# Layer-2 experts in two groups: selection of the second group between the first group's rows, sorted merges of quarters, b2 by a 16-bit product

## The chip, the cores and the metric

The kernel is one program for one core of a Trainium2 chip. The time is that of one execution on the device, in microseconds; the profile adds one execution in which the hardware recorded every instruction. Five engines run side by side and meet only through semaphores: TensorE (PE in the profile; its weight loads are listed apart as PEld), VectorE (DVE), ScalarE (ACT), GpSimd (POOL) and SyncE (SP), which here only issues DMAs.

## What is computed

The whole model is twelve residual blocks over 4096 tokens of 128 numbers. The change touches only the feed-forward block of layer 2, `l2_ffn`, which runs twice. Each of its 48 experts picks its own 128 best tokens out of all 4096:

```python
logits = xf @ Wr.T                                  # 4096 tokens x 48 experts
vals, idx = jax.lax.top_k(logits.T, cap)            # cap = 128, per expert
w = jax.nn.softmax(vals, axis=-1)
xg = xf[idx]
h = jax.nn.gelu(jnp.einsum('ecd,esdm->ecsm', xg, W1) + b1[:, None], approximate=False)
y = jnp.einsum('ecsm,esmk->ecsk', h, W2) + b2[:, None]      # s = 4 parts, k = 32 columns each
y = y.reshape(E, cap, D) * w[..., None]
out = jnp.zeros_like(xf).at[idx.reshape(-1)].add(y.reshape(-1, D))
```

`xf` is the layer norm of `x`, and the block adds half of `out` to `x`.

## The kernel before

`l2_ffn` has four stretches.

**Routing.** The layer norm of 8 chunks of 512 tokens is made on VectorE (`ln_dve`, L180), turned on TensorE (L190), kept by ScalarE (L196), and multiplied with the router's weights (L2105). ScalarE keeps the logits in `lt` (L2053): the experts lie on the partitions, tokens 0 to 2047 on partitions 0 to 47 and tokens 2048 to 4095 on partitions 64 to 111, so `lt` is 128 x 2048. The unused partitions are filled with a low number (L1961, L1962).

**Selection.** Sixteen rounds on VectorE, each of three passes over `lt`: the 8 largest (MAX8, L1969), their places (FIND_INDEX8, L1971), and their removal (MATCH_REPLACE8, L1973; not in the last round). The two halves of an expert are then merged: two small DMAs by SP bring the upper half beside the lower, one comparison picks 128 out of 256 (L1982 to L1990; this keeps the right set, in no order), ScalarE makes the exponentials (L2062), TensorE turns the lists (L2112, L2113), and VectorE writes the token numbers `from_i` and `to_i` (L1996 to L1998).

**Experts.** A pipeline over 48 experts. GpSimd gathers an expert's 128 rows (`gather`, L1935) four experts ahead and scatters the results with addition (L1947). TensorE's order in a step is `up(n + 1)`, `turn(n + 2)`, `down(n)`:

```python
pe.transpose(s.tp[:, 0, 0:P], xg[:, q, :], core.ident[:, :])                                  # turn, L2118
pe.matmul(hu[:, u, j * P:(j + 1) * P], w1[:, q, :, :].rearrange("p s m -> p (s m)")[:, j::S],  # up, L2126
          xgt[:, u, :], start=True, stop=True)
pe.matmul(yp[:, u, 0:D], h[:, u, j, :], w2b[:, q, j, :], start=j == 0, stop=j == S - 1)       # down, L2136
```

In `up` the weights of `w1` are read with a step of 4 elements (`j::S`). In `down` the activations `h` are the weights that are loaded, and 128 columns of `w2b` are moved through; `w2b` is W2 spread out with zeros by VectorE (`spread`, L2006), so that one product serves all four parts. ScalarE copies the turned rows (L2066) and applies GELU (L2073). VectorE adds b2 (L2013) and multiplies with the softmax weight (L2018); `keep` is these two. SP reloads the ring of four experts' weights (L1876, L1878) after each `down`.

**End.** SP reads both sums back in four pieces (L1904), VectorE adds them (L2035) and makes the statistics for the next block (L203).

Every wait is written by hand: `x.wait_ge(sig.sem, sig.past(n))` waits until the n-th event of that signal has happened.

## Time and profile before

| what | value |
|---|---|
| time, median of 3 runs | 3180.63 us (3173.9 to 3186.78) |
| the profiled execution's own time | 3173.69 us |
| its span | 3171.9 us |
| PE busy | 2425.3 us (76%) |
| DVE busy | 1559.8 us (49%) |
| ACT busy | 1072.4 us (34%) |
| POOL busy | 860.3 us (27%) |

Busy time is the union of an engine's instructions; the rest of the span the engine waits. These shares are means over blocks with different limits, so they say nothing of `l2_ffn` alone. The span is 1.8 us shorter than that execution's time: this much lies around it.

### The profile page before, as it was taken

To read this page: it belongs to the slowest core of one execution; us is meant where nothing else is said; L and a number is where in the kernel's file an instruction comes from. 1 tells how busy PE (TensorE), PEld (TensorE's weight loads), DVE (VectorE), ACT (ScalarE), POOL (GpSimd) and SP (SyncE) were. 2 spreads that over 40 slices of the span, in tenths; PEclk is the share of its full clock that TensorE was granted. 3 is DMA by queue.
4 is the path that set the end of the run, shared out by engine and by line. 5 is a ranking of instruction groups with operands and counts; after the bars stand their busy time and mean duration, and the time that the engine had idled before them with its cause. 6 is when DMAs were issued, how large, how long until landed. Compare 5 with 4: busy or idle time off the path is not lost. (4 is left out here: it accounts for less than half of the span.)

```text
span 3171.9 us, 45200 instructions
## 1 busy us (share of the span) xinstructions
PE 2425.3 (76%) x13236; PEld 1610.9 (51%) x13237; DVE 1559.8 (49%) x3705; ACT 1072.4 (34%) x2452; POOL 860.3 (27%) x784
## 2 busy tenths in 40 slices
PE   5979879665667313969999822968999688979998
PEld 3645556454546302955666612964444245544444
DVE  5749867544773597342334487342111577751110
ACT  1433234410341011634444311633222155662221
POOL 2535435365136402850000011851000122210000
PEclk9989879665875556989999855988999688989999
DMA  5110011457045631660000041661000333310000
GB/s 196 41 51 1 1 51 40 165 122 183 14 167 118 178 119 33 145 149 18 1 2 1 10 128 23 147 145 37 0 0 0 85 81 72 88 42 1 0 0 27
DMA packets 265331, 212.61 MB, mean 67 GB/s; under 512 B 56448, under 2 KB 245069, under 8 KB 262125
## 3 DMA queue, kind: packets, MB, share of 16 engines
q1 hardware_dynamic: 231021, 176.82, 18.8%
q0 software_dynamic: 34176, 34.09, 6.5%
q8 instruction: 73, 1.20, 0.2%
q14 instruction: 61, 0.50, 0.1%
HBM read 145.33 MB, written 64.91 MB: 66 GB/s over the span
## 5 line engine op out<-in xcount | busy, mean ns | idle before, releaser
L161 POOL TENSOR_TENSOR fields<-ln_t,power 128x4 f32<-128x4 f32 (+1 forms) x96 | 96.7, 1027 | 651.7 <-DVE ln_t L154 651.4
L2515 DVE TENSOR_TENSOR fields<-fields,s_y 128x512 f32 (+1 forms) x16 | 11.0, 687 | 496.8 <-PE s_y L2594 496.8
L2579 PE MATMUL s_z<-s_ha,s_wt_h 128*128 128x512 f32 x512 | 222.4, 592 | 0.0
L2586 PE MATMUL s_z<-s_hb,s_wt_h 128*128 128x512 f32 x512 | 222.3, 592 | 0.0
L2805 DVE TENSOR_REDUCE s_mx<-s_sa 128x2 f32<-128x512 f32 x256 | 167.1, 685 | 65.2 <-PE s_sa L2958 63.6
L2126 PE MATMUL s_hu<-s_xgt,s_w 128*128 128x128 f32 x768 | 195.4, 400 | 1.7 <-issue 1.7
L2886 ACT ACTIVATE s_e<-s_sc 128x512 f32<-128x512 f32 x256 | 149.9, 599 | 127.1 <-PE s_sc L2974 125.4
L2126 PEld LDWEIGHTS s_hu<-s_xgt,s_w 128*128 128x128 f32 x768 | 186.7, 327 | 3.0 <-issue 3.0
L2112 PE MATMUL s_lp<-ident,s_posf 48*128 48x48 f32 x2 | 0.6, 312 | 233.3 <-DVE s_prob L1994 233.3
L190 PE MATMUL s_tp<-ident,xn 128*128 128x128 f32 x288 | 60.6, 348 | 143.5 <-DVE xn L180 140.5
L1935 POOL DMA_INDIRECT s_xg<-rows_dram,s_from_i x96 | 95.5, 995 | 268.6 <-DVE s_to_i L1998 240.0
L1947 POOL DMA_INDIRECT acc_dram<-s_yo,s_to_i x96 | 153.3, 1597 | 41.6 <-issue 29.0
L2586 PEld LDWEIGHTS s_z<-s_hb,s_wt_h 128*128 128x128 f32 x512 | 97.4, 190 | 122.4 <-issue 122.4
L2579 PEld LDWEIGHTS s_z<-s_ha,s_wt_h 128*128 128x128 f32 x512 | 96.3, 190 | 115.7 <-issue 115.7
L2958 PE MATMUL s_sa<-s_kx,s_qx 72*128 72x256 bf16 x512 | 113.1, 308 | 39.1 <-DVE s_mx L2805 21.3
L190 PEld LDWEIGHTS s_tp<-ident,xn 128*128 128x128 f32 x288 | 44.1, 184 | 170.0 <-DVE xn L180 140.2
L2112 PEld LDWEIGHTS s_lp<-ident,s_posf 48*128 48x128 f32 x2 | 0.4, 180 | 234.9 <-issue 234.9
L2570 PE MATMUL s_z<-xnt,s_wt_w 128*128 128x512 f32 x256 | 112.7, 593 | 4.6 <-ACT s_wt_w L2529 4.6
L2013 DVE TENSOR_TENSOR s_yb<-s_yp,s_b 128x128 f32<-128x128 f32 x96 | 28.0, 291 | 175.5 <-issue 110.0
L2236 DVE TENSOR_SCALAR s_den<-s_kn 128x8 f32<-128x8 f32 x64 | 10.3, 160 | 210.9 <-PE s_kn L2397 210.9
L2226 POOL TENSOR_TENSOR s_rd<-s_rv,s_power 128x2 f32<-128x2 f32 x16 | 11.1, 697 | 371.6 <-DVE s_rv L2260 371.6
L196 ACT ACTIVATE xnt<-s_tp 128x512 f32<-128x512 f32 x72 | 43.0, 597 | 201.5 <-PE s_tp L190 193.6
(458 smaller groups left out, 6039.0 us busy)
## 6 DMA issues: line engine op xcount, KB each, us to landing
s_w<-in_L_ffn_W_dram SPq DMA_DIRECT2D x96, 256.0 KB
acc_dram<-s_zero SPq DMA_DIRECT2D x32, 512.0 KB, 5.9
s_kx<-k_dram SPq DMA_DIRECT2D x16, 576.0 KB
s_qx<-q_dram SPq DMA_DIRECT2D x48, 192.0 KB
fields<-acc_dram SPq DMA_DIRECT2D x16, 512.0 KB, 7.2
table_dram<-s_table_rows SPq DMA_DIRECT2D x2, 3136.0 KB, 9.2
s_wg<-in_L_ffn_w_gate_dram SPq DMA_DIRECT2D x64, 96.0 KB
s_wu<-in_L_ffn_w_up_dram SPq DMA_DIRECT2D x64, 96.0 KB
```

The costliest lines, as they stand in the source:

```text
L161: pool.tensor_tensor(core.rstd[:, tiles], core.ln_t[:, 2, tiles], core.power[:, 0:CT], ALU.pow).then_inc(s.scale_ready.sem, 1)
L190: last = pe.transpose(s.tp[:, u % s.tp_banks, j * P:(j + 1) * P], core.xn[:, u, j, :], core.ident[:, :])
L196: act.activation(core.xnt[:, u, :], s.tp[:, u % s.tp_banks, :], ACT.Copy).then_inc(s.xnt_ready.sem, 1)
L1935: pool.indirect_dma_start(xg[:, n % RING, :], None, table, bass.IndirectOffsetOnAxis(ap=from_i[:, n:n + 1], axis=0)).then_inc(xg_loaded[n ...
L1947: pool.indirect_dma_start(sums, bass.IndirectOffsetOnAxis(ap=to_i[:, n:n + 1], axis=0), yo[:, n % RING, :], None, compute_op=ALU.add).then ...
L2126: last = pe.matmul(hu[:, u, j * P:(j + 1) * P], w1[:, q, :, :].rearrange("p s m -> p (s m)")[:, j::S], xgt[:, u, :], start=True, stop=True)
L2570: pe.matmul(z[:, (2 * f + half) % 4, :], wt[m][:, 0, f * P:(f + 1) * P], core.xnt[:, u, :], start=True, stop=True).then_inc(group_done.sem, 1)
L2579: last = pe.matmul(z[:, o, :], wt["h1"][:, f, o * P:(o + 1) * P], ha[:, f, :], start=f == 0, stop=f == HB - 1)
L2586: last = pe.matmul(z[:, o, :], wt["h2"][:, f, o * P:(o + 1) * P], hb[:, f, :], start=f == 0, stop=f == HB - 1)
L2805: dve.tensor_reduce(mx[:, i, t, 2 * pairs:2 * pairs + 2], sa[:, n % 2, :, :], AX.X, ALU.max).then_inc(max_done.sem, 1)
L2886: act.activation(e[:, n % RING, :, :], sc[:, n % 2, :, :], ACT.Exp).then_inc(exp_done.sem, 1)
L2958: last = pe.matmul(sa[:, n % 2, a, :], qx[0:ROWS, slot, h, t * P:(t + 1) * P], kx[0:ROWS, slot, h, :], start=True, stop=True)
```

## The change

The router's logits are laid out anew: four quarters of 1024 tokens on partitions 0 to 31, 32 to 63, 64 to 95 and 96 to 127, for 32 experts at a time. So there are two groups, of 32 and of 16 experts (the second is padded with repeated experts up to 32), and two products a chunk in the routing. VectorE selects for group 0 in sixteen rounds over 128 x 1024, merges quarters pairwise by DMA, sorts the merged lists with a bitonic network of seven steps (`sort_step`; equal values go by token number), and merges once more. Then the experts start; the 47 passes and the merges of group 1 stand between the `keep`s of experts 0 to 29 in VectorE's order. GpSimd gathers the first four experts of group 1 at steps 30 and 31.

Besides this: W1 is loaded so that `up` reads its weights densely; W2 of all 48 experts is loaded once, in packets of 128 bytes, and `down` moves 32 columns a part with no spreading; b2 is split into three 16-bit parts and enters by one bf16 product of 3 rows; the normalized rows go straight to `all_xn` (GpSimd's copies L1923 go); loops are written out; and the rows of x, the table and the sums lie in DRAM partition by partition, so that their packets are 4 KB and more in place of 512 bytes.

```diff
+    LANES = 32
+    PARTS = P // LANES
+    PART = TOKENS // PARTS
+    GROUPS = ((0, LANES), (LANES, EXPERTS - LANES))
+    ROUNDS = CAP // TOP
+    STEPS = 7
     LOW = -3.0e38
...
+            def load(n):
+                sp.dma_start(w1[:, n % RING, :, :], w["L2_ffn_W1"][n].rearrange("s d m -> d s m")).then_inc(ring_loaded[n % RING].sem, 16)
...
+            with nc.allow_non_contiguous_dma("the second weights of a part of a row"):
+                for e in range(0, EXPERTS, 8):
+                    sp.dma_start(w2[:, e:e + 8, :, :].rearrange("p e s k -> p (e s) k"),
+                                 w["L2_ffn_W2"][e:e + 8].rearrange("e s m k -> m (e s) k")).then_inc(w2_loaded.sem, 16)
...
+                if n in (0, LANES):
+                    pool.wait_ge(index_ready.sem, index_ready.past(n // LANES))
...
-                if n + RING < EXPERTS:
+                if n + RING < LANES or LANES <= n < EXPERTS - RING:
                     gather(n + RING)
+                if n == LANES - 2:
+                    gather(LANES)
+                    gather(LANES + 1)
+                if n == LANES - 1:
+                    gather(LANES + 2)
+                    gather(LANES + 3)
...
+            def round_part(g, k):
+                r = k // 3
+                got = lists[:, 0, r * TOP:(r + 1) * TOP]
+                data = lt[:, g, :, :].rearrange("p i w -> p (i w)")
+                if k % 3 == 0:
+                    dve.max(got, data)
+                    dve.drain()
+                if k % 3 == 1:
+                    dve.max_index(pos[:, r * TOP:(r + 1) * TOP], got, data)
+                if k % 3 == 2 and r < ROUNDS - 1:
+                    dve.match_replace(data, got, data, LOW)
+                    dve.drain()
...
+            def sort_step(j):
+                n = 3 * LANES
+                far = CAP // 2 >> j
+
+                def half(buf, field, side):
+                    return merge[0:n, buf, field, :].rearrange("p (b two w) -> p b two w", two=2, w=far)[:, :, side, :]
+
+                def wide(t, which=0):
+                    return t[0:n, which * (CAP // 2):(which + 1) * (CAP // 2)].rearrange("p (b w) -> p b w", w=far)
+
+                a, b = j % 2, 1 - j % 2
+                va, vb, pa, pb = half(a, 0, 0), half(a, 0, 1), half(a, 1, 0), half(a, 1, 1)
+                dve.tensor_tensor(wide(level), va, vb, ALU.is_equal)
+                dve.tensor_tensor(wide(before), pa, pb, ALU.is_lt)
+                dve.tensor_tensor(wide(above), va, vb, ALU.is_gt)
+                dve.tensor_tensor(wide(step), pa, pb, ALU.subtract)
+                dve.drain()
+                dve.tensor_tensor(wide(level), wide(level), wide(before), ALU.mult)
+                dve.tensor_tensor(half(b, 0, 0), va, vb, ALU.max)
+                dve.tensor_tensor(half(b, 0, 1), va, vb, ALU.min)
+                dve.drain()
+                dve.tensor_tensor(wide(above), wide(above), wide(level), ALU.add)
+                dve.drain()
+                dve.tensor_tensor(wide(step), wide(step), wide(above), ALU.mult)
+                dve.drain()
+                dve.tensor_tensor(half(b, 1, 0), pb, wide(step), ALU.add)
+                last = dve.tensor_tensor(half(b, 1, 1), pa, wide(step), ALU.subtract)
+                if j == STEPS - 1:
+                    last.then_inc(sorted_ready.sem, 1)
+                dve.drain()
...
+            def keep(n):
+                u = n % 2
+                dve.wait_ge(y_done.sem, y_done.past(n))
+                if n >= RING:
+                    dve.wait_ge(added[u].sem, 16 * ((n - RING) // 2 + 1))
+                dve.tensor_scalar(yo[:, n % RING, :], lp[:, u, 0:D], prob_s[:, n:n + 1], None, ALU.mult).then_inc(y_kept.sem, 1)
...
+            dve.wait_ge(logits_kept.sem, logits_kept.past(1))
+            for k in range(3 * ROUNDS):
+                round_part(0, k)
+            put_lists()
+            merge_pairs(0)
+            for j in range(STEPS):
+                sort_step(j)
+            merge_last(0)
+            weigh(0)
+            place(0)
+            dve.drain()
+            dve.wait_ge(logits_kept.sem, logits_kept.past(3))
+            for n in range(EXPERTS):
+                keep(n)
+                for k in range(min(9 * n // 4, 3 * ROUNDS), min(9 * (n + 1) // 4, 3 * ROUNDS)):
+                    round_part(1, k)
+                if n == 21:
+                    put_lists()
+                if n == 22:
+                    merge_pairs(1)
+                    sort_step(0)
+                if n == 23:
+                    sort_step(1)
+                    sort_step(2)
...
-            def spread(n, ring, q):
-                dve.wait_ge(ring_loaded[q].sem, ring * 32 + 32)
-                dve.wait_ge(y_done.sem, y_done.past(n - RING))
-                dve.tensor_tensor(w2b[:, q, :, :].rearrange("p j (s k) -> p j s k", s=S),
-                                  w2[:, q, :, :].unsqueeze(2).to_broadcast([P, S, S, K]),
-                                  own[:, :].unsqueeze(1).unsqueeze(3).to_broadcast([P, S, S, K]), ALU.mult).then_inc(w2_spread.sem, 1)
...
-                pe.matmul(lp[:, u, :], wr[:, :], core.xnt[:, u, :], start=True, stop=True).then_inc(routed.sem, 1)
...
+                for g in range(2):
+                    last = pe.matmul(lp[lanes, 2 * g + c % 2, :], wr[:, g * LANES:(g + 1) * LANES], core.xnt[:, c % 2, :],
+                                     start=True, stop=True)
+                last.then_inc(routed.sem, 1)
...
-                    last = pe.matmul(hu[:, u, j * P:(j + 1) * P], w1[:, q, :, :].rearrange("p s m -> p (s m)")[:, j::S],
-                                     xgt[:, u, :], start=True, stop=True)
+                    last = pe.matmul(hu[:, u, j * P:(j + 1) * P], w1[:, n % RING, j, :], xgt[:, u, :], start=True, stop=True)
...
-                pe.wait_ge(w2_spread.sem, w2_spread.past(n))
+            def down(n):
+                u = n % 2
                 pe.wait_ge(gelu_done.sem, gelu_done.past(n))
-                pe.wait_ge(y_kept.sem, y_kept.past(n - 2))
+                if n >= 2:
+                    pe.wait_ge(y_kept.sem, y_kept.past(n - 2))
+                pe.matmul(lp[:, u, 0:D], ones_b[:, :], b2[:, n, :], start=True, stop=False)
                 for j in range(S):
-                    last = pe.matmul(yp[:, u, 0:D], h[:, u, j, :], w2b[:, q, j, :], start=j == 0, stop=j == S - 1)
+                    last = pe.matmul(lp[:, u, j * K:(j + 1) * K], h[:, u, j, :], w2[:, n, j, :], start=False, stop=j == S - 1)
                 last.then_inc(y_done.sem, 1)
...
+                if n == 28:
+                    turn_slots(1)
```

TensorE's order in the middle of the expert pipeline. `s_xg` is the gathered rows, `s_hu` the output of `up`, `s_yp` (before) and `s_lp` (after) that of `down`; the shapes are those of the output. Before, a step and a bit:

```order
L2126 MATMUL s_hu<-s_xgt,s_w 128x128 x4
L2118 MATMUL s_tp<-ident,s_xg 128x128
L2136 MATMUL s_yp<-s_w2b,s_h 128x128 x4
L2123 REGISTER_ALU
L2126 MATMUL s_hu<-s_xgt,s_w 128x128 x4
```

Of the change:

```order
L2270 MATMUL s_hu<-s_xgt,s_w 128x128 x4
L2261 MATMUL s_tp<-ident,s_xg 128x128
L2278 MATMUL s_lp<-s_b,s_ones_b 128x128
L2280 MATMUL s_lp<-s_w,s_h 128x32 x4
L2270 MATMUL s_hu<-s_xgt,s_w 128x128 x4
```

The order of the step is the same; each `down` has one product more, and its four large ones write 32 columns in place of 128.

VectorE's order in the experts. Before, `keep` is two instructions and `spread` one:

```order
L2006 TENSOR_TENSOR s_w2b<-s_w,s_own 128x512
L2013 TENSOR_TENSOR s_yb<-s_yp,s_b 128x128
L2018 TENSOR_SCALAR s_yo<-s_yb,s_prob_s 128x128
L2006 TENSOR_TENSOR s_w2b<-s_w,s_own 128x512
L2013 TENSOR_TENSOR s_yb<-s_yp,s_b 128x128
```

Of the change, from the end of group 0's lists on (`s_lists` and `s_lt` are the lists and the logits of a group):

```order
L2104 TENSOR_SCALAR s_to_i<-s_lp 128x16
L2112 TENSOR_SCALAR s_yo<-s_lp,s_prob_s 128x128
L2015 MAX s_lists<-s_lt 128x8
L2018 MAX_INDEX s_pos<-s_lists,s_lt 128x8
L2112 TENSOR_SCALAR s_yo<-s_lp,s_prob_s 128x128
L2020 MATCH_REPLACE s_lt<-s_lists,s_lt 128x1024
L2015 MAX s_lists<-s_lt 128x8
L2112 TENSOR_SCALAR s_yo<-s_lp,s_prob_s 128x128
L2018 MAX_INDEX s_pos<-s_lists,s_lt 128x8
L2020 MATCH_REPLACE s_lt<-s_lists,s_lt 128x1024
```

`keep` is one instruction now, and two or three passes over group 1's logits stand behind each of them, up to expert 21; the merges follow at experts 21 to 29.

TensorE's order in the routing, the end of a chunk; before and then of the change:

```order
L190 MATMUL s_tp<-ident,xn 128x128 x4
L2105 MATMUL s_lp<-xnt,s_wr 128x512
```

```order
L2231 MATMUL s_tp<-ident,all_xn 128x128 x4
L2242 MATMUL s_lp<-xnt,s_wr 32x512 x2
```

A chunk has two products of 512 moving columns where it had one.

## Rows read from the trace of the kernel before

**Rows 1.** Stretches (from:to, length): routing, selection, lists, experts, end; the second execution whole

```profile
core 0: us, PE busy (x) PEld busy (x) DVE busy (x) ACT busy (x) POOL busy (x), PEclk, DMA share, GB/s
1101.60:1124.40 22.80, 16.10 (x55) 8.47 (x55) 15.03 (x41) 9.70 (x19) 14.09 (x20) 0.68 0.87 279
1124.40:1235.10 110.70, 0.00 (x0) 0.00 (x0) 108.31 (x79) 1.30 (x2) 0.00 (x0) 0.51 0.14 41
1235.10:1241.60 6.50, 0.42 (x2) 0.29 (x2) 2.75 (x15) 0.50 (x2) 0.02 (x1) 0.50 0.04 10
1241.60:1402.70 161.10, 146.54 (x816) 141.07 (x816) 57.66 (x144) 92.61 (x262) 124.29 (x96) 0.96 0.61 129
1402.70:1422.30 19.60, 0.00 (x0) 0.00 (x0) 11.48 (x36) 0.00 (x0) 0.00 (x0) 0.50 0.85 214
1819.20:2141.30 322.10, 163.55 (x873) 149.39 (x873) 196.12 (x314) 104.24 (x284) 138.68 (x116) 0.74 0.47 111
```

**Rows 2.** Timeline, POOL in the experts: start us, us, engine, line, op, count, [idle before <-releaser]

```profile
1306.92 0.98 POOL L1935 DMA_INDIRECT s_xg<-rows_dram,s_from_i  x1 [0.30 <-PE s_tp L2118]
1308.21 1.59 POOL L1947 DMA_INDIRECT acc_dram<-s_yo,s_to_i  x1 [0.30 <-issue]
```

**Rows 3.** Timeline, weight loads of one step of the experts at the full clock

```profile
1254.95 1.95 PEld L2126 LDWEIGHTS s_hu<-s_xgt,s_w 128*128 128x128 f32 x8
1256.69 0.27 PEld L2118 LDWEIGHTS s_tp<-ident,s_xg 128*128 128x128 f32 x1
1256.92 0.97 PEld L2136 LDWEIGHTS s_yp<-s_w2b,s_h 128*128 128x128 f32 x8
1257.82 0.31 PEld L2126 LDWEIGHTS s_hu<-s_xgt,s_w 128*128 128x128 f32 x1
```

**Rows 4.** Timeline, the end: a sum over 1024 columns on VectorE

```profile
1408.66 1.22 DVE L2035 TENSOR_TENSOR fields<-fields,s_acc_b 128x1024 f32<-128x1024 f32 x1 [9.86 <-DMA s_acc_b<-acc_dram]
```

**Rows 5.** Timeline, from the lists to the first gather and the first turn

```profile
1238.04 0.28 DVE L1982 TENSOR_TENSOR s_first<-s_vals 48x128 f32<-48x128 f32 x1 [2.50 <-DMA s_posf<-s_posf]
...
1238.52 0.28 DVE L1985 TENSOR_TENSOR s_posf<-s_posf 48x128 f32<-48x128 f32 x1
1238.87 0.28 DVE L1987 TENSOR_TENSOR s_posf<-s_posf,s_first 48x128 f32<-48x128 f32 x1
...
1241.58 1.09 POOL L1935 DMA_INDIRECT s_xg<-rows_dram,s_from_i  x1 [119.85 <-DVE s_to_i L1998]
...
1244.25 0.18 PEld L2118 LDWEIGHTS s_tp<-ident,s_xg 128*128 128x128 f32 x1 [3.55 <-DMA s_xg<-rows_dram,s_from_i]
```

**Rows 6.** Timeline, layer 1: an element by element operation on 64 columns

```profile
724.96 0.22 DVE L1375 TENSOR_TENSOR s_hp<-s_gs,s_gu 96x64 f32<-96x64 f32 x1 [1.77 <-issue]
```

**Rows 7.** Timeline, the router's product at the full clock: two records, one product

```profile
1117.52 1.02 PE L2105 MATMUL s_lp<-xnt,s_wr 128*128 128x512 f32 x2
```

**Rows 8.** Timeline, weight loads at the low clock: expert 0's `down`, and layer 0's router

```profile
1250.40 1.78 PEld L2136 LDWEIGHTS s_yp<-s_w2b,s_h 128*128 128x128 f32 x8 [0.34 <-issue]
...
390.74 1.83 PEld L664 LDWEIGHTS s_yp<-s_wr,xnt 128*128 128x128 f32 x8
392.31 0.90 PEld L190 LDWEIGHTS s_tp<-ident,xn 128*128 128x128 f32 x4
393.19 1.83 PEld L664 LDWEIGHTS s_yp<-s_wr,xnt 128*128 128x128 f32 x8
```

**Rows 9.** The same view as rows 1: layer 0's router, layer 1's experts, layer 2's experts

```profile
389.00:406.00 17.00, 16.22 (x81) 15.96 (x79) 7.67 (x32) 4.26 (x8) 4.99 (x6) 0.50 0.32 132
700.00:760.00 60.00, 48.08 (x246) 44.53 (x246) 21.87 (x74) 8.27 (x38) 48.43 (x39) 0.50 0.67 140
1252.60:1314.00 61.40, 58.83 (x336) 57.07 (x336) 23.96 (x60) 38.61 (x107) 49.28 (x38) 1.00 0.67 146
```

**Rows 10.** Page, the DMA queue of SP: packets, MB, share of 16 engines

```profile
q1 hardware_dynamic: 231021, 176.82, 18.8%
```

**Rows 11.** Timeline, ScalarE at the start of the experts

```profile
1245.06 1.28 ACT L2066 ACT_TABLE_LOAD   x1
```

More of the change, by code:

```diff
@@ L1892, in _ @@
[L1892 to L1899 removed]
+                tiles = slice(n * 8, (n + 1) * 8)
+                sp.dma_start(region_rows(1)[:, tiles, :], zero[:, :, :]).then_inc(zeroed.sem, 16)
@@ new lines, in move, with move2 @@
+            def move(g):
+                sp.wait_ge(best_found.sem, best_found.past(g))
+                sp.dma_start(other[0:LANES, :, :], lists[LANES:2 * LANES, :, :]).then_inc(moved.sem, 16)
+                sp.dma_start(other[2 * LANES:3 * LANES, :, :], lists[3 * LANES:P, :, :]).then_inc(moved.sem, 16)
+            def move2(g):
+                sp.wait_ge(sorted_ready.sem, sorted_ready.past(g))
+                sp.dma_start(other2[:, :, :], merge[2 * LANES:3 * LANES, 1, :, :]).then_inc(moved2.sem, 16)
@@ L1900, in _ @@
+            move(0)
+            move2(0)
+            for n in range(EXPERTS - RING):
+                sp.wait_ge(y_done.sem, y_done.past(n))
+                load(n + RING)
+                if n == 20:
+                    move(1)
+                if n == 26:
+                    move2(1)
             for q in range(2):
@@ L2026, in _, with normal @@
-            dve.wait_ge(b2_loaded.sem, 16)
-            spread(0, 0, 0)
-            ring_body(0, False)
-            with dve.Fori(1, EXPERTS // RING - 1) as ring:
-                ring_body(ring)
-            ring_body(EXPERTS // RING - 1, last=True)
+            def normal(c):
+                dve.wait_ge(s.scale_ready.sem, s.scale_ready.past(c))
+                for t in range(c * CT, (c + 1) * CT):
+                    last = dve.tensor_scalar(core.all_xn[:, t, :], core.x[:, t, :], core.mean[:, t:t + 1], core.rstd[:, t:t + 1],
+                                             ALU.subtract, ALU.mult)
+                last.then_inc(xn_ready.sem, 1)
@@ new lines, in _ @@
+            dve.drain()
+            dve.tensor_copy(offset[:, :], offset_i[:, :])
+            for c in range(2, CHUNKS):
+                normal(c)
+            cut_b2()
+            dve.wait_ge(logits_kept.sem, logits_kept.past(1))
[8 more added lines that the diff above has]
+            place(0)
@@ L2072, in gelu @@
                 for j in range(S):
-                    last = act.activation(h[:, u, j, :], hu[:, u, j * P:(j + 1) * P], ACT.Gelu, bias=b1[:, j, bass.ds(n, 1)])
+                    last = act.activation(h[:, u, j, :], hu[:, u, j * P:(j + 1) * P], ACT.Gelu, bias=b1[:, j, n:n + 1])
                 last.then_inc(gelu_done.sem, 1)
-            turn(0, 0)
-            def ring_body(n0, last=False):
-                for q in range(RING):
-                    if not (last and q == RING - 1):
-                        turn(n0 + q + 1, q + 1)
-                    gelu(n0 + q, q)
@@ L2084, in _ @@
-            with act.Fori(0, EXPERTS // RING - 1) as ring:
-                ring_body(ring * RING)
-            ring_body(EXPERTS - RING, True)
+            exp(0)
+            turn(0)
+            for n in range(EXPERTS):
+                if n + 1 < EXPERTS:
+                    turn(n + 1)
+                gelu(n)
+                if n == 28:
+                    exp(1)
         @block.tensor
@@ new lines, in turn_slots, with turn @@
+            def turn_slots(g):
+                pe.wait_ge(listed.sem, listed.past(g))
+                for a in range(2):
+                    last = pe.transpose(slots(g)[:, a, :], final[:, a, :], core.ident[0:LANES, 0:LANES])
+                last.then_inc(slots_turned.sem, 1)
+            pe.wait_ge(logits_kept.sem, logits_kept.past(3))
+            turn_slots(0)
+            pe.wait_ge(b2_placed.sem, 48)
+            pe.wait_ge(w2_loaded.sem, 16 * (EXPERTS // 8))
+            def turn(n):
+                pe.wait_ge(xg_loaded[n % RING].sem, 16 * (n // RING + 1))
+                if n >= 1:
+                    pe.wait_ge(xt_kept.sem, xt_kept.past(n - 1))
+                pe.transpose(tp[:, 0, 0:P], xg[:, n % RING, :], core.ident[:, :]).then_inc(xt_done.sem, 1)
@@ L2151, in _ @@
-            with pe.Fori(0, EXPERTS // RING - 1) as ring:
-                ring_body(ring * RING, ring)
-            ring_body(EXPERTS - RING, EXPERTS // RING - 1, True)
+            turn(0)
+            up(0)
+            turn(1)
+            for n in range(EXPERTS):
+                if n + 1 < EXPERTS:
+                    up(n + 1)
+                if n + 2 < EXPERTS:
+                    turn(n + 2)
+                down(n)
+                if n == 28:
+                    turn_slots(1)
 def l2_attn(core):
```

356 lines of the change are left out of this document (179 added, 177 removed).

## The prediction

> **What bounds the kernel now.** I read the stretches first, since the page's shares mix blocks with different limits. An execution of `l2_ffn` takes 320.7 us of the span (1101.6 to 1422.3) and the second 322.1 [rows 1]: 643 of 3171.9 us. Each stretch has one limit. In the selection VectorE works 108.3 of 110.7 us, alone. The lists are a chain of 6.5 us between engines. In the experts (161.1 us) both TensorE and GpSimd are nearly full, 146.5 and 124.3 us. The timeline then shows the two loops: GpSimd needs 0.30 + 0.98 for a gather and 0.30 + 1.59 for a scatter, 3.17 us an expert [rows 2]; TensorE at its full clock needs 2.87 us, from 1254.95 to 1257.82, of which `up` takes 1.74, `turn` 0.23 and `down` 0.90 [rows 3]. So GpSimd sets the pace, with TensorE close behind, as long as the clock is at its upper level: the stretch has a granted share of 0.96 [rows 1].
>
> **Selection.** The 108.3 us are 47 passes of 2.30 us over 2048 columns [rows 1]. The trace has no pass over 1024 columns. Another VectorE operation takes 1.22 us for 1024 [rows 4], as a column per cycle with a small fixed part would, so I take 1.24 for a pass. Group 0 costs 47 x 1.24 plus the gaps that stay (2.4 us), 60.7 us: **-50 us** an execution. The bounds are 1.15 (half of 2.30) and 1.35.
>
> **Lists of group 0.** 6.5 us now. New are seven sort steps, one merge and one more move by DMA. A step has eleven operations on 96 x 64, 0.22 us each [rows 6], with five drains; a dependent operation starts its own length + 0.07 after the last one's start (1238.52 to 1238.87) [rows 5], and independent ones overlap a little. That is 2.3 us, 16.2 for seven. A second move costs about what the first does, 2.50 us of waiting [rows 5]; the second merge with its index arithmetic about twelve operations of 0.2, 2.5. Together **+21 us**, between 16 and 26. Nothing hides it.
>
> **Routing.** VectorE loses the low fills, GpSimd its copies, but TensorE has two products of 512 columns a chunk in place of one. A product is two records in 1.02 us, a little less in a row since the last one's tail overlaps [rows 7]; eight more are some 7 us at the upper clock, and TensorE was busy 16.1 of 22.8 us [rows 1]. I take **+5 us**, from +2 to +9 by how early the clock rises.
>
> So the first gather comes 24 us earlier. Up to here the change gains.
>
> **Experts, GpSimd and VectorE.** GpSimd's 3.17 us stay. VectorE gets, for 22 experts, 2.25 passes x 1.24 + 0.3 for `keep` = 3.1, with drains 3.2 us; `spread` goes. The passes are queued ahead of the next `keep`, three of them at worst 3.8 us, and `down(n + 2)` and the scatter wait for a `keep`, but with two experts of slack. Neither gives a pace above 3.3 us.
>
> **Experts, TensorE, the term that decides.** At the upper clock dense weights bring `up` from 1.74 to 0.90 as `down` has [rows 3]; `down` keeps its 0.90, since its eight weight loads stay although it moves a quarter of the columns, and gets one bf16 product (0.1). That is 2.1 us, no longer a limit. But this stretch starts after VectorE's long stretch alone, at the low level. There `down` needs 1.78 us for its eight loads [rows 8], 0.21 to 0.22 each. That a load with few columns behind it costs the same at this level, layer 0's router shows: eight loads with 8 moving columns and four with 128 take 2.45 us, 0.204 each (390.74 to 393.19) [rows 8]. So at 1.2 GHz: 8 x 0.213 for `up`, 8 x 0.213 for `down`, 0.23 for `turn`, 0.12 for the bias: **3.76 us an expert**, above the 3.17 of GpSimd. The new loop is slower than the old one unless the clock rises.
>
> Does it? Before, it does: from 1252.6 on the share is 1.00, with TensorE busy 58.8 of 61.4 us and 128 columns moved per 128-column load [rows 9]. In layer 0's router TensorE is as full, 16.2 of 17.0 us, but eight of twelve loads have 8 columns behind them, and the share stays 0.50 through the stretch; in layer 1's experts it stays 0.50 for 60 us, TensorE busy 48.1, with 64 columns in half its products [rows 9]. The new loop is of that kind: half of its loads have 32 columns behind them. I take it that the clock stays at 1.2 GHz.
>
> The Trainium skill (TensorE: Matmul & The Clock Gate, Why this matters for your kernels) says that keeping TensorE continuously busy brings the full clock. Here the trace differs: 16.2 of 17.0 us busy went with 0.50 [rows 9]. By the page the pace would be GpSimd's, and the sum that of the first rival below.
>
> **Sum of the experts at the low clock.** First gather to first turn 2.7 us (1241.58 to 1244.25) [rows 5], 0.9 more to `up(0)`, 48 x 3.76 = 180.5, about 1.5 for the first experts' dependences, and 4.6 from the last `down` to the stretch's end, both as now. The change of groups costs a hole: `turn_slots(1)` waits for `weigh(1)`, which waits for an exponential behind `gelu(28)` with its table load of 1.28 us and another back to GELU [rows 11], then `place(1)`, the gather (2.7 us) and `turn(32)`: some 4.5 us of idle TensorE at expert 29 and 3.5 at 30, together 8, where nothing covers it. Total 198 against 161.1: **+37 us**.
>
> **End.** Packets of 4 KB in place of 512 bytes; VectorE works only 11.5 of 19.6 us there [rows 1]. **-2 us**, between 0 and -5.
>
> **Sum.** -50 + 21 + 5 + 37 - 2 = +11 us an execution, +21 us for two: 3173.7 + 21 = 3195 on the profiled execution's own time. That one lies 7 us under the median of 3180.6, which gives 3202; I say **3200 us**.
>
> **Rivals.**
> *The clock rises in the new loop* (0.14). For it: the loop before it did so, and TensorE would be full at the low level. Against it: [rows 9]. Then GpSimd and VectorE set 3.2 us, and with the hole the experts are some 9 us longer than now: -50 + 21 + 5 + 9 - 2 = -17 an execution, 3145 us. This is the case on the other side. The sign turns at 3.76 - 11/48 = 3.53 us an expert.
> *VectorE or the 128-byte packets of W2 bind* (0.08). A pass over 1024 that took 1.6 us would make 22 experts 0.3 us slower than the 3.76 and add 17 us to the selection: some 22 an execution, 3244 us. W2 has 24,576 packets, 1536 for each of 16 engines; the queue's mean is 41 ns a packet (0.188 x 16 x 3171.9 us / 231021) [rows 10], which gives 63 us from the routing's end on, some 1126, as group 0's lists are done at 1124.4 + 5 + 60.7 = 1190. It binds from 42 ns for the first move in the same queue, and from 58 ns for the first turn; at 80 ns it would cost some 33 us an execution, 3266. Smaller packets should take less than the mean.
> *It gains nothing and loses nothing* is the lower half of the likeliest case: a pace of 3.6 us and short lists.
>
> **Numbers.** Low clock 0.78, of it range 3175 to 3228 (pace 3.7 to 3.95, lists and routing +-5 each). A measurement of this kernel can tell about 0.5%, 16 us. Low clock: slower 0.48, same 0.28, faster 0.02. High clock: faster 0.14. The binding rival: slower 0.06, same 0.02. Together slower 0.54, same 0.30, faster 0.16. The range 3148 to 3230 holds most of the low case and the upper half of the fast one.
>
> **What would show it.** In the profile after: PEclk 0.5 through the experts; `up` and `down` weight loads of 0.21 us spacing; steps of 3.8 us with GpSimd waiting for VectorE's `yo`, VectorE for TensorE; the first gather 24 us earlier; passes of 1.24 us; a hole of 8 us near expert 30. It is wrong if the share is 1.0 there: then steps of 3.2 us and a time near 3145.

## The result, and the profile after

The changed kernel takes **3215.7 us** (median of 4 runs, 3209.5 to 3216.6), the kernel before, run beside it, 3182.0 us (3173.9 to 3186.8): a ratio of 1.0112, 95% interval 1.0093 to 1.0130. It is 34 us, about 1.1%, slower, which is more than the 0.5% a measurement can tell. The forecast was 3200 us, slower, with a range of 3148 to 3230. The profiled executions stand further apart, 3213.7 against 3171.9 us of span, since that of before, 3173.7 us, was faster than all four runs.

The stretches of the first execution of `l2_ffn` after, which begins 2.7 us later in the span than before: routing, group 0's selection, its lists, experts, end; the last row is the second execution whole. They answer to [rows 1].

```profile
core 0: us, PE busy (x) PEld busy (x) DVE busy (x) ACT busy (x) POOL busy (x), PEclk, DMA share, GB/s
1104.30:1131.10 26.80, 22.25 (x69) 7.67 (x69) 11.26 (x46) 6.52 (x14) 9.64 (x12) 0.82 0.85 285
1131.10:1191.60 60.50, 0.00 (x0) 0.00 (x0) 58.17 (x78) 2.22 (x3) 0.00 (x0) 0.53 0.55 51
1191.60:1219.40 27.80, 0.39 (x2) 0.28 (x2) 18.33 (x101) 0.49 (x2) 0.00 (x0) 0.50 0.02 4
1219.40:1431.50 212.10, 200.20 (x866) 177.89 (x866) 91.18 (x227) 67.49 (x245) 123.45 (x96) 0.50 0.42 85
1431.50:1448.90 17.40, 0.00 (x0) 0.00 (x0) 11.48 (x36) 0.00 (x0) 0.00 (x0) 0.50 0.75 242
1842.00:2186.40 344.40, 222.65 (x937) 185.84 (x937) 190.47 (x487) 76.73 (x263) 132.99 (x108) 0.53 0.46 96
```

| us, one execution | before | after | difference | forecast |
|---|---|---|---|---|
| routing | 22.8 | 26.8 | +4.0 | +5 |
| selection (group 0) | 110.7 | 60.5 | -50.2 | -50 |
| lists (group 0) | 6.5 | 27.8 | +21.3 | +21 |
| experts | 161.1 | 212.1 | +51.0 | +37 |
| end | 19.6 | 17.4 | -2.2 | -2 |
| sum | 320.7 | 344.6 | +23.9 | +11 |

The second execution went from 322.1 to 344.4, +22.3. The two give 46 us; the spans differ by 42, so the other blocks of this one execution were 4 us shorter, which I leave as what single executions differ by.

The experts' granted share fell from 0.96 [rows 1] to 0.50. A step of their loop after, weight loads alone (each row: start, length, engine, line, tile, shape, count, idle time before):

```profile
1263.17 1.83 PEld L2270 LDWEIGHTS s_hu<-s_xgt,s_w 128*128 128x128 f32 x8
1264.88 0.23 PEld L2261 LDWEIGHTS s_tp<-ident,s_xg 128*128 128x128 f32 x1
1265.44 0.10 PEld L2278 LDWEIGHTS s_lp<-s_b,s_ones_b 3*128 3x128 bf16 x1 [0.33 <-issue]
1265.65 1.78 PEld L2280 LDWEIGHTS s_lp<-s_w,s_h 128*128 128x128 f32 x8
1267.31 1.83 PEld L2270 LDWEIGHTS s_hu<-s_xgt,s_w 128*128 128x128 f32 x8
```

A step is 1267.31 - 1263.17 = **4.14 us**, where the forecast had 3.76: `up` 1.71, from `turn` to the bias 0.56, from the bias to `down` 0.21, `down` 1.66. The engines behind TensorE wait in each step. GpSimd waits for `s_yo`:

```profile
1264.15 1.59 POOL L1983 DMA_INDIRECT acc_dram<-s_yo,s_to_i  x1 [1.31 <-DVE s_yo L2112]
...
1267.61 0.35 DVE L2112 TENSOR_SCALAR s_yo<-s_lp,s_prob_s 128x128 f32<-128x128 f32 x1 [1.24 <-PE s_lp L2280]
```

and VectorE, even with passes queued, waits for `down` (the second row is a `keep`). The waits run back to TensorE, which is busy without a gap. Here are fifty us out of the loop:

```profile
1240.00:1290.00 50.00, 50.00 (x220) 44.58 (x218) 37.10 (x60) 15.74 (x60) 31.19 (x25) 0.50 0.46 97
```

TensorE's row is 50.00 of 50.00 us and the granted share still 0.50.

The selection and the lists went as worked out. A pass over 1024 columns takes 1.21 to 1.23 us, a round of three passes 3.85 (1131.10 to 1134.95), and a sort step 2.46 (1196.22 to 1198.68) in place of 2.3, which is 1 us more for seven that the rest of the lists gave back. The wait for the first move, 2.52 us, is the 2.50 of [rows 5], so W2's packets did not hold it up:

```profile
1131.10 1.23 DVE L2015 MAX8 s_lists<-s_lt 128x8 f32<-128x1024 f32 x1 [12.89 <-ACT s_lt L2179]
...
1134.95 1.23 DVE L2015 MAX8 s_lists<-s_lt 128x8 f32<-128x1024 f32 x1
...
1194.73 0.29 DVE L2031 TENSOR_TENSOR s_above<-s_lists,s_other 96x128 f32<-96x128 f32 x1 [2.52 <-DMA s_other<-s_lists]
...
1196.22 0.22 DVE L2057 TENSOR_TENSOR s_level<-s_merge 96x64 f32<-96x64 f32 x1
...
1198.68 0.22 DVE L2057 TENSOR_TENSOR s_level<-s_merge 96x64 f32<-96x64 f32 x1
```

The group change, by TensorE's weight loads from the `up` of expert 29 on:

```profile
1341.83 1.83 PEld L2270 LDWEIGHTS s_hu<-s_xgt,s_w 128*128 128x128 f32 x8
...
1347.08 0.29 PEld L2249 LDWEIGHTS s_tp<-ident,s_final 32*128 32x128 f32 x2 [0.99 <-DVE s_final L2095]
1347.43 1.78 PEld L2270 LDWEIGHTS s_hu<-s_xgt,s_w 128*128 128x128 f32 x8
...
1351.53 1.83 PEld L2270 LDWEIGHTS s_hu<-s_xgt,s_w 128*128 128x128 f32 x8
1356.92 0.18 PEld L2261 LDWEIGHTS s_tp<-ident,s_xg 128*128 128x128 f32 x1 [3.57 <-DMA s_xg<-rows_dram,s_from_i]
...
1359.20 0.97 PEld L2270 LDWEIGHTS s_hu<-s_xgt,s_w 128*128 128x128 f32 x4
```

The `up`s stand 5.60, 4.10 and 7.67 us apart (the view ends inside the last one, so that it shows only four of its eight loads). Over 4.14 that is 1.5 for the turn of the lists and 3.5 for the first gather: 5.0 us in all, not 8.

### The profile page after: what moved, and what is told of

Same layout as the page of the kernel before. It is cut to its first block and busy times, and to the rows that moved or that the text cites. A ratio compares the mean times of both kernels' runs of the same rounds, so it can differ in the third digit from the quotient of the medians.

```text
span 3213.7 us, 44096 instructions
## 1 busy us (share of the span) xinstructions
PE 2542.3 (79%) x13364; PEld 1682.2 (52%) x13365; DVE 1552.8 (48%) x4051; ACT 1017.8 (32%) x2410; POOL 848.2 (26%) x768
## 5 line engine op out<-in xcount | busy, mean ns | idle before, releaser
L161 POOL TENSOR_TENSOR fields<-ln_t,power 128x4 f32<-128x4 f32 x96 | 96.5, 1031 | 648.2 <-DVE ln_t L154 648.2
L2280 PE MATMUL s_lp<-s_w,s_h 128*128 128x32 f32 x768 | 183.9, 404 | 0.0
L2280 PEld LDWEIGHTS s_lp<-s_w,s_h 128*128 128x128 f32 x768 | 170.9, 327 | 11.2
L2270 PEld LDWEIGHTS s_hu<-s_xgt,s_w 128*128 128x128 f32 x768 | 175.1, 333 | 3.2 <-issue 3.1
L190 PE MATMUL s_tp<-ident,xn 128*128 128x128 f32 x224 | 46.4, 344 | 131.9 <-DVE xn L180 130.1
L2112 DVE TENSOR_SCALAR s_yo<-s_lp,s_prob_s 128x128 f32<-128x128 f32 x96 | 33.7, 351 | 225.7 <-PE s_lp L2280 223.6
L2197 ACT ACTIVATE s_xgt<-s_tp 128x128 f32<-128x128 f32 x96 | 26.6, 277 | 271.7 <-PE s_tp L2261 271.7
L2205 ACT ACTIVATE s_h<-s_hu,s_b 128x128 f32<-128x128 f32 x384 | 109.2, 374 | 5.3 <-PE s_hu L2270 5.2
```

The source lines that it names most:

```text
L161: pool.tensor_tensor(core.rstd[:, tiles], core.ln_t[:, 2, tiles], core.power[:, 0:CT], ALU.pow).then_inc(s.scale_ready.sem, 1)
L2205: last = act.activation(h[:, u, j, :], hu[:, u, j * P:(j + 1) * P], ACT.Gelu, bias=b1[:, j, n:n + 1])
L2270: last = pe.matmul(hu[:, u, j * P:(j + 1) * P], w1[:, n % RING, j, :], xgt[:, u, :], start=True, stop=True)
L2280: last = pe.matmul(lp[:, u, j * K:(j + 1) * K], h[:, u, j, :], w2[:, n, j, :], start=False, stop=j == S - 1)
```

## The experiments

What was open: whether the clock, and the 32 columns, are the cause (theory A) or VectorE, GpSimd and the group change would hold the loop at that length anyway (B); and what makes the step 4.14 and not 3.76 us. The table puts them together. "Experts" is from the first gather to the first load of the end stage, with its granted share, in the first execution.

| kernel | median us | ratio to before (95%) | experts us | share |
|---|---|---|---|---|
| after | 3215.7 | 1.0112 (1.0093-1.0130) | 212.1 | 0.50 |
| e1_wide | 3144.9 | 0.9889 (0.9859-0.9919) | 173.8 | 0.88 |
| e2_before_narrow | 3243.5 | 1.0181 (1.0136-1.0226) | 190.0 | 0.50 |
| e4_no_bias | 3181.5 | 1.0008 (0.9991-1.0026) | 190.4 | 0.50 |
| e5_passes_ahead | 3307.8 | 1.0399 (1.0369-1.0429) | 257.8 | 0.50 |
| e6_diag | 3149.9 | 0.9887 (0.9851-0.9924) | 174.1 | 0.88 |
| e7_before_dense | 3182.3 | 0.9986 (0.9963-1.0009) | 161.6 | 0.93 |
| e8_diag_order | 3146.2 | 0.9861 (0.9823-0.9899) | 173.2 | 0.87 |
| e9_fp32_bias | 3263.4 | 1.0252 (1.0203-1.0302) | 224.1 | 0.55 |
| e10_rows128 | 3185.0 | 1.0009 (0.9991-1.0027) | 198.8 | 0.50 |
| e11_wide_start | 3201.2 | 1.0070 (1.0047-1.0093) | 203.6 | 0.55 |
| e12_earlier | 3147.8 | 0.9898 (0.9860-0.9935) | 171.8 | 0.91 |
| e13_move_later | 3141.0 | 0.9874 (0.9854-0.9894) | 170.8 | 0.88 |

### e1_wide: the same products, 128 columns wide

```diff
-                    last = pe.matmul(lp[:, u, j * K:(j + 1) * K], h[:, u, j, :], w2[:, n, j, :], start=False, stop=j == S - 1)
+                    last = pe.matmul(lp[:, u, 0:D], h[:, u, j, :], w2[:, n, :, :], start=False, stop=j == S - 1)
```

> The changed kernel, but each product of `down` moves the whole 128 columns of its expert's W2 and adds them into the whole 128 columns of `s_lp`, in place of its own part's 32 into its own 32. So the sum over the parts is another computation than the reference's; loads, products and waits are as many as in the changed kernel. Theory A (the 32 columns keep TensorE's clock at 1.2 GHz, and the clock sets the pace): the granted share goes to 1.00 after the first experts, a step from 4.14 to some 3.2 us (GpSimd's 3.17), the experts from 212 to about 168 us, the whole to about 3128 us. Theory B (VectorE's passes, GpSimd or the group change hold the loop anyway): the share may rise, but the stretch stays within 10 us of 212 and the time within 3195 to 3215 us. Theory C (nothing moves the clock here, and wide products only cost): no change, 3215 us.

Measured 3144.9 us, 71 less than the changed kernel for moving four times the columns in `down`. A's direction and mechanism hold, its size is 17 us too hopeful. The loads and GpSimd in the loop:

```profile
1266.91 0.14 PEld L2261 LDWEIGHTS s_tp<-ident,s_xg 128*128 128x128 f32 x1 [0.95 <-DMA s_xg<-rows_dram,s_from_i]
1267.17 0.09 PEld L2278 LDWEIGHTS s_lp<-s_b,s_ones_b 3*128 3x128 bf16 x1
1267.33 0.97 PEld L2280 LDWEIGHTS s_lp<-s_w,s_h 128*128 128x128 f32 x8
1268.21 0.97 PEld L2270 LDWEIGHTS s_hu<-s_xgt,s_w 128*128 128x128 f32 x8
```

```profile
1267.58 0.99 POOL L1965 DMA_INDIRECT s_xg<-rows_dram,s_from_i  x1 [0.30 <-PE s_tp L2261]
1268.87 1.59 POOL L1983 DMA_INDIRECT acc_dram<-s_yo,s_to_i  x1 [0.30 <-issue]
1270.77 0.99 POOL L1965 DMA_INDIRECT s_xg<-rows_dram,s_from_i  x1 [0.31 <-issue]
```

Both `up` and `down` take 0.89 us, TensorE waits for a gather, and GpSimd goes from one gather to the next in 3.19 us with no wait beyond its 0.30: the limit has changed hands. What A had left out stands in the windows of the same stretch:

```profile
1226.00:1290.00 64.00, 52.67 (x373) 45.02 (x372) 60.34 (x95) 26.49 (x102) 50.64 (x40) 0.96 0.59 126
1290.00:1325.00 35.00, 23.01 (x149) 19.56 (x149) 23.55 (x110) 14.03 (x48) 22.17 (x17) 0.88 0.50 98
1325.00:1350.00 25.00, 18.87 (x110) 16.46 (x110) 2.41 (x10) 7.99 (x32) 15.94 (x13) 0.77 0.43 94
```

In 1226 to 1290 GpSimd is busy 50.6 of 64 us, which is full at its 0.30 per instruction, and VectorE is nearly as full, 60.3; from 1290 to 1350 GpSimd is not, and the share dips. That is where VectorE merges group 1's lists between `keep`s and where the groups change.

### e2_before_narrow: the columns alone, in the old kernel

```diff
-                    last = pe.matmul(yp[:, u, 0:D], h[:, u, j, :], w2b[:, q, j, :], start=j == 0, stop=j == S - 1)
+                    last = pe.matmul(yp[:, u, j * K:(j + 1) * K], h[:, u, j, :], w2b[:, q, j, j * K:(j + 1) * K], start=True, stop=True)
```

> The kernel before, but each product of `down` moves only the 32 columns of its part's block in `s_w2b` and writes them to its part's 32 columns; `spread` and everything else stay, and the result is the same. Theory A: the granted share stays at 0.50 through the experts; a step is `up` 1.80 + `turn` 0.60 + `down` 1.66 = 4.06 us as at expert 0 of the kernel before, the stretch 161 becomes about 206 us, the time about 3180 + 90 = 3270 us. Theory B: less is moved, TensorE's weight loads stay 0.90 for `down` at the upper clock, and the time stays at 3180 us.

3243.5 us, 63 us more than before for a quarter of the columns, at a share of 0.50 throughout. The step is 3.76 us (1257.22 to 1260.98):

```profile
1257.22 0.25 PEld L2118 LDWEIGHTS s_tp<-ident,s_xg 128*128 128x128 f32 x1
1257.45 1.83 PEld L2136 LDWEIGHTS s_yp<-s_w2b,s_h 128*128 128x128 f32 x8
1259.16 1.97 PEld L2126 LDWEIGHTS s_hu<-s_xgt,s_w 128*128 128x128 f32 x8
1260.98 0.25 PEld L2118 LDWEIGHTS s_tp<-ident,s_xg 128*128 128x128 f32 x1
```

A foresaw 4.06, with 0.60 for `turn` as at expert 0 of the kernel before. In the running loop `turn` takes 0.23; the 0.34 us at expert 0 is no part of it. Theory B, by which less work can't cost, falls. With e1 this shows the cause from both sides: in the old loop and in the new one the share is 0.50 with 32 columns behind half of the loads, and 0.96 and 0.88 with 128 (e9 and e11 below have a short exception at the start of the experts).

### e5_passes_ahead: VectorE's passes out of the loop

```diff
             dve.wait_ge(logits_kept.sem, logits_kept.past(3))
+            for k in range(3 * ROUNDS):
+                round_part(1, k)
+            put_lists()
             for n in range(EXPERTS):
                 keep(n)
-                for k in range(min(9 * n // 4, 3 * ROUNDS), min(9 * (n + 1) // 4, 3 * ROUNDS)):
-                    round_part(1, k)
-                if n == 21:
-                    put_lists()
```

> The changed kernel with all 47 passes of group 1 done before the first `keep` in place of between the `keep`s of experts 0 to 20; the merges stay where they are. GpSimd and TensorE start as before and run into the buffers' limits after a few experts, so some 60 us are added ahead. Theory A (TensorE at the low clock sets the pace): the step stays 4.14 us from then on, and the time is about 3215 + 2 x 55 = 3325 us. Theory B (VectorE's passes set or share the pace of the first 21 experts): their step falls well below 4.14 once the passes are gone, by up to 0.9 us each, and the time is about 3290 us.

3307.8 us, 92 more, with the stretch 45.7 us longer. The step without passes is 4.14 us as with them (`turn` at 1292.13 and 1296.27), and TensorE is full again:

```profile
1290.00:1340.00 50.00, 50.00 (x220) 44.62 (x219) 4.21 (x12) 15.74 (x60) 31.82 (x25) 0.50 0.48 97
```

So in the changed kernel the passes cost the steps nothing, and standing between them they save 46 us an execution. The time alone would not decide: 3307.8 us lies halfway between A's 3325 and B's 3290, but the step is A's. My estimate of 55 took too little off for the three experts that TensorE does ahead.

### e4_no_bias, e9_fp32_bias, e10_rows128: the missing 0.38 us

e4 drops the product `ones_b` x `b2`. e9 makes `b2` one row of 32 bits, e10 128 rows of 16 bits:

```diff
-        b2 = s.sb("b2", [3, EXPERTS, D], BF16)
-        ones_b = s.sb("ones_b", [3, P], BF16)
+        b2 = s.sb("b2", [P, EXPERTS, D], BF16)
+        ones_b = s.sb("ones_b", [P, P], BF16)
```

> The changed kernel without the 16-bit product of the bias (b2 is left out of the result; the four parts of `down` each start their own columns). Theory D (the 0.33 us in which TensorE stands idle in each step comes with the 16-bit product): a step goes from 4.14 to 4.14 - 0.21 - 0.33 = 3.60 us, 26 us less an execution, about 3163 us. Theory E (the idle time stands behind `turn`, whatever comes next, as at expert 0 of the kernel before, where a transposition at 1.2 GHz took 0.60 us up to the next load): only the product's 0.21 go, step 3.93, about 3195 us. In both the clock stays at 0.50.

> The changed kernel, but the bias enters by one 32-bit product of one row (a row of ones and b2 as it is) in place of one 16-bit product of three rows. Without a bias product the step was 3.63 us, with the 16-bit one 4.14. Theory D (the idle 0.33 us comes with the change between 32 and 16 bits): the step is 3.63 + two weight loads of 0.21 = 4.05 us, about 3206 us. Theory H (any small extra product brings the idle time): 4.38 us, about 3238 us.

> The changed kernel, but the 16-bit product of the bias has 128 rows in place of 3 (rows 3 to 127 are zeros), so it loads and moves full height. An execution pays some us more ahead of the experts for the fill. Theory I (the idle time comes with the step from 128 rows to few and back): the step is 3.63 + 0.1 to 0.2 = 3.75 to 3.85 us. Theory D (it comes with the change to 16 bits): the step stays 4.14 us. The granted share stays 0.50 in both.

e4: the step is 3.63 us (`turn` at 1262.16 and 1265.79), the idle time is gone with the product, and the time is that of the kernel before. D was right on the step and E fell. On the time D missed: it had 3163 us, and 3181.5 lies between that and E's 3195. A part of this stands in the trace: the stretch is 21.7 us shorter and not 26, since the two steps of the group change now cost 7.5 us over the others, where they cost 5.1 in the changed kernel. The rest is the spread of this kernel's runs, 3171 to 3190 us, of which the profiled one is the fastest.

e9 refutes D's reason. Its product is of 32 bits like its neighbours, and the step is 4.65 us (1261.18 to 1265.83), longer than D's 4.05 and than H's 4.38, with idle time on both sides:

```profile
1261.18 0.23 PEld L2261 LDWEIGHTS s_tp<-ident,s_xg 128*128 128x128 f32 x1
1261.75 0.50 PEld L2278 LDWEIGHTS s_lp<-s_b,s_ones_b 1*128 1x128 f32 x2 [0.33 <-issue]
1262.47 1.78 PEld L2280 LDWEIGHTS s_lp<-s_w,s_h 128*128 128x128 f32 x8 [0.23 <-issue]
```

e10 has the 16 bits but full height, and no idle time:

```profile
1263.53 0.23 PEld L2263 LDWEIGHTS s_tp<-ident,s_xg 128*128 128x128 f32 x1
1263.74 0.15 PEld L2280 LDWEIGHTS s_lp<-s_b,s_ones_b 128*128 128x128 bf16 x1
1263.96 1.83 PEld L2282 LDWEIGHTS s_lp<-s_w,s_h 128*128 128x128 f32 x8
1265.67 1.83 PEld L2272 LDWEIGHTS s_hu<-s_xgt,s_w 128*128 128x128 f32 x8
1267.37 0.23 PEld L2263 LDWEIGHTS s_tp<-ident,s_xg 128*128 128x128 f32 x1
```

Its step is 3.84 us. Theory I holds for the three rows: with the type as it was and 128 rows, the idle time is gone and the step 0.30 us shorter. That one row of 32 bits pays for the same reason is likely, but no run fills it up, so its part isn't shown. The 125 rows of zeros save 31 us of the whole (3185.0 against 3215.7).

### e11_wide_start: does the clock stay up once it is up?

As e1_wide for `n < 6` alone, the narrow products from 6 on.

> The changed kernel with the wide products (128 columns, every part into the whole output: another computation of the same size for these experts) for the experts 0 to 5 alone, and the narrow ones from 6 on. Theory A: the clock rises during the first experts as it did with wide products throughout, and falls back to 1.2 GHz some experts after the narrow ones begin; from there the step is 4.14 us, and the whole gains 5 to 20 us on 3215. Rival (once up, the clock stays up as long as TensorE has work): about 3145 us.

3201.2 us, 15 less. Consecutive stretches:

```profile
1235.00:1245.00 10.00, 8.42 (x64) 7.10 (x62) 9.48 (x16) 4.17 (x16) 8.17 (x7) 1.00 0.62 132
1245.00:1255.00 10.00, 8.23 (x43) 7.07 (x43) 9.56 (x17) 3.73 (x15) 8.17 (x7) 0.68 0.63 118
1255.00:1265.00 10.00, 10.00 (x46) 9.10 (x45) 7.43 (x12) 2.82 (x11) 6.60 (x7) 0.50 0.47 93
1265.00:1300.00 35.00, 35.00 (x154) 30.97 (x153) 26.39 (x41) 11.06 (x43) 22.17 (x18) 0.50 0.46 99
```

The first narrow `down` begins at 1245.86, and by 1249.86 its loads are at the low level's spacing again. But the wide products did not start this rise: the share leaves 0.50 between 1228 and 1229, and the first wide `down` begins at 1229.48. e9, narrow throughout, has the same rise in its first execution:

```profile
1227.00:1247.00 20.00, 18.23 (x134) 15.72 (x132) 16.94 (x27) 9.80 (x38) 13.94 (x11) 1.00 0.52 113
1248.00:1443.00 195.00, 186.83 (x762) 164.25 (x762) 73.09 (x200) 55.26 (x203) 104.15 (x80) 0.50 0.40 79
```

e10 and e5 have one of 10 and 6 us at the start of their second executions; the changed kernel, e2 and e4 have none. Why some executions rise there and others don't stays open. What all the narrow ones share is that the share, once down, stays at 0.50 to the end of the experts, while in e6, which has wide products, it dips at the group change and is back at 1.00 from 1337 to 1343. So the rival falls: a high clock did not last with narrow products. What the six wide experts themselves were worth isn't shown.

### e7_before_dense: what dense weights bring alone

```diff
-                    last = pe.matmul(hu[:, u, j * P:(j + 1) * P], w1[:, q, :, :].rearrange("p s m -> p (s m)")[:, j::S],
+                    last = pe.matmul(hu[:, u, j * P:(j + 1) * P], w1[:, q, j, :],
```

> The kernel before, but `up` reads its weights densely, w1[:, q, j, :] in place of every fourth column (so hidden units are paired with other rows of W2: another computation of the same size). Theory F (GpSimd's 3.17 us set the step at the full clock): TensorE's step falls from 2.87 to about 2.05 us, and the time stays within 5 us of 3180. Theory G (TensorE had a share in the step): the stretch of 161 us loses some 0.2 us an expert, about 3160 us.

3182.3 us, no difference, as F said. TensorE's busy time fell from 146.5 [rows 1] to 109.8 us, GpSimd's stayed at 124.3, and the stretch at 161.6. The share was 0.93 with 128 columns behind every load, though TensorE was idle for a third of the time; in e2, with 32 behind half of them, it was 0.50 with TensorE busy 182.0 of 190.0 us. So in these runs the share does not go by how long TensorE is busy:

```profile
1242.04:1403.67 161.63, 109.76 (x816) 100.09 (x816) 58.11 (x144) 92.40 (x262) 124.27 (x96) 0.93 0.63 128
```

### e6_diag, e8_diag_order, e12_earlier, e13_move_later: a version that is faster

e6 gives the reference's result with wide products: GpSimd zeroes the slots at the start, and zeros stand beside each block of W2.

```diff
-        w2 = s.sb("w2", [P, EXPERTS, S, K])
+        w2 = s.sb("w2", [P, RING, S * (D + K)])
...
+                    sp.dma_start(w2[:, n % RING, :].rearrange("p (s d) -> p s d", s=S)[:, :, 0:K],
+                                 w["L2_ffn_W2"][n].rearrange("s m k -> m s k")).then_inc(ring_loaded[n % RING].sem, 16)
...
-                    last = pe.matmul(lp[:, u, j * K:(j + 1) * K], h[:, u, j, :], w2[:, n, j, :], start=False, stop=j == S - 1)
+                    last = pe.matmul(lp[:, u, 0:D], h[:, u, j, :], w2[:, n % RING, j * D:(j + 1) * D], start=False, stop=j == S - 1)
```

e8, in TensorE's loop (`LANES` is 32):

```diff
+                if n == LANES - 1:
+                    down(n)
                 if n + 1 < EXPERTS:
                     up(n + 1)
+                if n == LANES - 2:
+                    down(n)
                 if n + 2 < EXPERTS:
                     turn(n + 2)
-                down(n)
+                if n not in (LANES - 2, LANES - 1):
+                    down(n)
```

e12, VectorE's part, and SP's, where e13 has 19 in place of 17:

```diff
-                for k in range(min(9 * n // 4, 3 * ROUNDS), min(9 * (n + 1) // 4, 3 * ROUNDS)):
+                for k in range(min(5 * n // 2, 3 * ROUNDS), min(5 * (n + 1) // 2, 3 * ROUNDS)):
...
+                if 19 <= n < 19 + STEPS:
+                    sort_step(n - 19)
...
-                if n == 20:
+                if n == 17:
                     move(1)
```

> The changed kernel with W2 in a ring of four experts, loaded with W1 of the same expert (in packets of 128 bytes) into the diagonal blocks of zeroed slots, so that each product of `down` moves 128 columns, of which 96 are zeros, and the result is the reference's. By theory A as the kernel with wide products showed it: the clock goes to 1.00 in the experts, the stretch takes about 174 us, and the time is 3145 us. If the packets of 128 bytes of each expert don't land within a step (3.2 us), TensorE waits for the weights and the time is above 3180 us.

> The kernel of e6_diag, and in TensorE's order `down` of experts 30 and 31 stands ahead of the `turn` of experts 32 and 33, so that these two scatters don't wait for group 1's first gather. Expected: the hole at the group change gets some 4 us shorter, 8 us less than e6_diag in all, about 3137 us. If the chain from the exponential to the gather sets the hole alone, it stays as in e6_diag.

> The kernel of e6_diag with group 1's work brought forward: 2.5 passes behind each `keep` in place of 2.25, one sort step behind each of the experts 19 to 25, the last merge, the exponential, the turn and the placing one expert earlier each, and the gathers of experts 32 and 33 at step 29. The first 19 experts then go at VectorE's pace (2.5 x 1.24 + 0.35 + gaps = 3.6 us in place of 3.2, 8 us more), and the merges, which in e6_diag held the scatters up from expert 22 on, fit into GpSimd's step. Expected: the index of group 1 some 12 us earlier, the hole gone, 5 us less an execution, about 3138 us. Rival: what is gained at the group change is lost in the first 19 experts, 3148 us.

> The kernel of e12_earlier, but in SP's order the move of group 1's lists stands behind the weight load issued at step 19 in place of step 17. In e12_earlier SP's queue stood at that move from 1287.8 to 1298.1 us, with the loads of three experts behind it, and TensorE waited 6.06 us for weights at expert 22. Expected: that wait is gone, 5 us less an execution, about 3138 us. Rival: GpSimd, which had waited only 3.6 us there, catches up anyway and the time stays within 3 us of 3148.

e6 came as expected, 3149.9 us: 66 us below the changed kernel and 1.1% below the one before. e8, 3146.2, can't be told from it, and its stretch is 0.9 us shorter, not 4: the chain to group 1's gather holds. In e12 the hole at the group change shrank (8.0 us between two `turn`s in e6, 1324.96 to 1332.99; here the `up`s are at most 5.8 apart, 1320.68 to 1326.44), but the time stayed. Two losses stand against the gain. From the `turn` of expert 0 to that of expert 19, where each `keep` has 2.5 passes behind it, e12 takes 63.1 us and e6 58.3, as the rival said. And SP's queue stood at the move of group 1's lists, with the weights of three experts behind it:

```profile
1287.27 0.51 SPq L1907 DMA_DIRECT2D s_w<-in_L_ffn_W_dram  x1
1298.14 0.52 SPq L1926 DMA_DIRECT2D s_other<-s_lists  x1
```

```profile
1303.20 1.78 PEld L2258 LDWEIGHTS s_hu<-s_xgt,s_w 128*128 128x128 f32 x8 [6.06 <-DMA s_w<-in_L_ffn_W_dram]
```

e13 moves it two steps back. That wait is gone from its trace, but it was worth only about 1 us: from the `turn` of expert 0 to that of expert 32 e13 takes 112.4 us and e12 113.4, since TensorE now waits for gathers (3.1 us before the `turn` at 1304.49, 2.5 before that at 1309.74). The stretches say the same, 170.8 against 171.8. The 5 us an execution that I expected aren't shown: 3141.0 us (0.9874, 0.9854 to 0.9894) is the lowest median of the study, but its interval and e12's overlap, and the rival, by which GpSimd catches up anyway, fits the trace better. That e13 beats both kernels, by 1.3% and 2.3%, is shown.

## Why the prediction was right, and where its terms were off

**What bounds the kernel before: right.** GpSimd sets the pace there: e7 takes 37 us of work from TensorE and the time doesn't move.

**Selection -50, lists +21, routing +5, end -2: right**, with -50.2, +21.3, +4.0 and -2.2. The estimate of 1.24 us for a pass was 0.02 above the rows.

**The clock stays at 1.2 GHz: right, and shown.** It was argued from [rows 9] alone, by likeness; e1 and e2 change only the columns, and the share follows each time. In the changed kernel itself it is 0.50 through the experts of both executions. The forecast's reason does not cover the rises at the start that e9, e10 and e5 have. The Trainium skill (TensorE: Matmul & The Clock Gate, Why this matters for your kernels) has it that continuous work brings the full clock. By that rule the time would have been the first rival's 3145 us. The trace doesn't agree: 50.00 of 50.00 us busy went with 0.50. The rival's time was well priced, though: e1 and e6, which do have the clock, measured 3145 and 3150 us.

**The step of 3.76 us: the mis-sized term.** "0.12 for the bias" was the product's own length. With it comes 0.3 us of idle time because it has 3 rows. From `turn` to `down` 0.77 us passed in place of 0.35, and 48 x 0.38 = 18 us an execution. Without the bias the step was 3.63 us against the forecast's 3.64. This term alone is why the kernel is slower rather than equal: e10, with full height and the clock as low, takes 3185.0 us against 3179.3 for the kernel before, a ratio of 1.0009.

**The hole of 8 us: 5.0.** I had charged 4.5 us to the turn of the lists; it cost 1.5, since most of the exponential's chain (its table loaded at 1341.39, itself at 1345.01) ran beside `down` of expert 28. That hangs on the step: counted by the `turn`s, the same two steps cost 5.1 us over the others here, 5.9 at 3.84 us a step (e10) and 7.5 at 3.63 (e4), so for its own step of 3.76 the forecast was nearer than the 5.0 says.

**Sum.** +18 for the step, -3 for the hole and -1 for the rest make the experts +51 in place of +37, and an execution +24 in place of +11. For both executions that is 46 in place of 21 us, 25 more, and the median is 16 above the forecast: the other blocks were 4 us shorter, the 7 us between profiled execution and median, which the forecast carried over, weren't there after the change (3215.5 and 3215.7), and rounding 3202 to 3200 took 2 the other way.

**Where luck helped.** The step of 4.14 us lies outside the 3.7 to 3.95 that the forecast gave the low clock. With it and all else as forecast, the sum is 3202 + 96 x 0.38 = 3238 us, above the range; the smaller hole, the other blocks and those 7 us brought the time back inside. The sign was helped too: e10, whose step of 3.84 us is the nearest to the forecast's, can't be told from the kernel before. So "slower" came true by way of the mis-sized term.

**The binding rival: excluded** for VectorE by e5 and by passes of 1.22 us, and for W2's packets by the 2.52 us of the first move. W2 had landed long before: the DMA engines moved 145 GB/s from 1140 to 1150, 25 from 1150 to 1160 and nothing from 1160 to 1190, where the forecast's 41 ns a packet would have kept them busy until 1189. Its bound for the first `turn` was also a little off: its own figures (1126, and 1190 + 27.7 + 2.7 = 1220) give 61 ns a packet and not 58.
